# A gated recurrence on one core: the second half's scan of m and tanh moved ahead of z's add and sigmoid

## The reference, cut to what matters

```python
def step(h, x_t):
    fused = jax.nn.sigmoid(jnp.concatenate([x_t, h], axis=-1) @ w_W + w_b)
    hidden_state, output_state = jnp.split(fused, 2, axis=-1)
    memory_state = x_t @ wx_W + wx_b + hidden_state * (h @ wh_W + wh_b)
    h_new = output_state * h + (1.0 - output_state) * jnp.tanh(memory_state)
    return (h_new, h_new)
_, hs = jax.lax.scan(step, h0, xT)
x = x + jnp.swapaxes(hs, 0, 1)
```

## Time and profile before

| what | value |
|---|---|
| time, median of 3 runs | 1808.27 us (1807.4 to 1808.76) |
| the profiled execution | 1807.97 us, its span 1806.1 us |
| granted TensorE clock | 0.998 over the span |
| PE, PEld, DVE, ACT, POOL busy | 99%, 90%, 64%, 46%, 20% of the span |

### The profile page before, as it was taken

How to read it: one execution, slowest core, us unless ns; L and a number is a source line. 1 busy time by engine, 2 the same in 40 slices (tenths; PEclk the granted TensorE clock), 3 DMA queues, 4 the chain that set the end, 5 groups by cost and what they waited for, 6 DMA issues and landing times.

```text
span 1806.1 us, 178513 instructions
## 1 busy us (share of the span) xinstructions
PE 1787.5 (99%) x78208; PEld 1629.9 (90%) x78208; DVE 1160.5 (64%) x6153; ACT 824.9 (46%) x3983; POOL 357.1 (20%) x1540
## 2 busy tenths in 40 slices
PE   7999999999999999999999999999999999999998
PEld 6999999999999999999999999999999999999997
DVE  2666666666666666666666666666666666666665
ACT  2444444444444444444444444444444444444444
POOL 0222222222222222222222222222222222222221
PEclk9999999999999999999999999999999999999999
DMA  6222333223332223332233322233322333223332
GB/s 218 87 67 86 91 91 91 73 75 91 91 91 85 69 86 92 92 92 69 81 92 92 91 77 74 88 91 91 91 68 80 91 91 92 74 74 94 92 92 82
DMA packets 180731, 159.86 MB, mean 89 GB/s; under 512 B 12016, under 2 KB 179440, under 8 KB 180720
## 3 DMA queue, kind: packets, MB, share of 16 engines
q1 hardware_dynamic: 180720, 159.72, 29.6%
HBM read 151.28 MB, written 8.39 MB: 88 GB/s over the span
## 4 chain that ended last, share of the span: by engine, by line
PE 98%; SPq 1%; DMA 0%; issue 0%; DVE 0%; ACT 0%; POOL 0%; POOLq 0%; DVEq 0%
PE ps L232 78%; PE ps L200 20%; SPq L167 0%; SPq L162 0%; DMA x_sb<-in_x 0%; SPq L153 0%; SPq L159 0%; DVE turned L324 0%; SPq L150 0%; DVE h L347 0%; DVE m_pre L338 0%; SPq L157 0%; SPq L156 0%; SPq L155 0%; DVE pre_r L328 0%
## 5 line engine op out<-in xcount | busy, mean ns | idle before, releaser
L232 PE MATMUL ps<-wh,h 128*8 128x128 f32 (+1 forms) x65536 | 1504.7, 246 | 2.6 <-issue 2.2
L232 PEld LDWEIGHTS ps<-wh,h 128*8 128x8 f32 x65536 | 1324.7, 90 | 143.1 <-DVE h L347 113.5
L324 DVE STREAM_TRANSPOSE turned<-ps 128x128 f32<-128x128 f32 (+1 forms) x2048 | 550.4, 269 | 412.4 <-PE ps L232 412.4
L277 ACT ACTIVATE m_by<-pre_r 128x16 f32<-128x16 f32 x1024 | 224.2, 219 | 701.2 <-DVE pre_r L328 701.2
L200 PE MATMUL ps<-x_next,wx_step 128*32 128x128 f32 x12288 | 433.0, 274 | 0.6 <-issue 0.6
L347 DVE TENSOR_TENSOR_SCAN h<-h_by,h 128x48 f32<-128x48 f32 x1024 | 274.2, 268 | 152.4 <-ACT h L286 152.4
L403 POOL TENSOR_TENSOR add<-turned,bias_h 128x16 f32<-128x16 f32 x1024 | 222.8, 218 | 709.9 <-DVE turned L324 681.5
L281 ACT ACTIVATE h_by<-pre_z 128x16 f32<-128x16 f32 x1024 | 229.6, 224 | 249.8 <-DVE pre_z L332 246.0
L200 PEld LDWEIGHTS ps<-x_next,wx_step 128*32 128x32 f32 x12288 | 316.1, 110 | 16.2 <-issue 4.3
L416 POOL TENSOR_TENSOR y<-x_sb,h 128x32 f32 x512 | 134.0, 262 | 734.5 <-DVE h L347 734.5
L286 ACT ACTIVATE h<-m_pre 128x32 f32<-128x32 f32 x1024 | 237.8, 232 | 1.8 <-DVE m_pre L338 1.8
(11 more groups left out here) (8 smaller groups left out, 1.1 us busy)
## 6 DMA issues: line engine op xcount, KB each, us to landing
wx_step<-in_w_x SPq DMA_DIRECT2D x516, 192.0 KB, 2.4
x_next<-in_x SPq DMA_DIRECT2D x132, 256.0 KB, 3.2
x_sb<-in_x SPq DMA_DIRECT2D x34, 256.0 KB, 3.2
out_h<-y SPq DMA_DIRECT2D x32, 256.0 KB, 2.9
wx<-in_w_x SPq DMA_DIRECT2D x6, 512.0 KB, 7.3
wh<-in_w_h SPq DMA_DIRECT2D x4, 768.0 KB, 11.0
bias_x<-in_b_x SPq DMA_DIRECT2D x1, 6.0 KB, 3.2
bias_h<-in_b_h SPq DMA_DIRECT2D x1, 2.0 KB, 3.6
```

Source lines behind the costliest of these rows:

```text
L232: mm = pe.matmul(ps[Q * j:Q * j + B, bank, 0:cols], h_of(s - 1, k), wh[:, k, j, at:at + cols], start=(k == 0), stop=(k == KC - 1), tile_po ...
L277: act.activation(m_by[:, o, :, 1], pre_r[:, o, :], ACT.Sigmoid).then_inc(r_ready[o], 1)
L324: return dve.transpose(turned[:, o, g0:g1].rearrange("p g c q -> p (g c) q"), ps[:, bank, 0:cols].rearrange("p (c q) -> p c q", q=Q))
```

## The change

1. **VectorE, half 1.** `mix_m(1)` goes ahead of the wait for Z_B's transpose and of `sum_z(1)`.
2. **ScalarE, half 1.** `new(1)` (tanh) goes ahead of `update(1)` (z's sigmoid).
3. **VectorE, first transpose.** In every fourth step the wait for RM_A now comes first and that for `y_added` second.
4. **TensorE, x products.** The wait for `x_next_loaded` is gone; SyncE instead waits for x before it loads the slot's weights, and issues x ahead of them, so that the weights' arrival stands for both. One semaphore for emptied banks becomes three, one for each bank, and the values that TensorE waits for are worked out once in 4 steps.
5. **ScalarE, last step of a block.** It waits for three semaphores in place of one, and adds three times in place of once.

```diff
--- before.py
+++ after.py
@@ -130,7 +130,7 @@
         h_ready = halves("h_ready")
         x_placed = sem("x_placed")
         hm_ready = halves("hm_ready")
-        xg_ready = sem("xg_ready")
+        xg_free = [sem(f"xg_free{u}") for u in range(X_UNITS)]
         xg_turned = sem("xg_turned")
 
         y_added = sem("y_added")
@@ -163,8 +163,10 @@
                     .then_inc(wx_step_loaded[s % RING], 16)
 
             for r in range(RING):
+                sp.dma_start(x_next[:, r], x_flat[:, :, TOK:2 * TOK]).then_inc(x_next_loaded[r], 16)
+            for r in range(RING):
+                sp.wait_ge(x_next_loaded[r], 16)
                 load_wx(r)
-                sp.dma_start(x_next[:, r], x_flat[:, :, TOK:2 * TOK]).then_inc(x_next_loaded[r], 16)
             sp.dma_start(x_sb[:, :, TOK:2 * TOK], x_flat[:, :, TOK:2 * TOK]).then_inc(x_loaded, 16)
             with sp.Fori(0, BLOCKS) as i:
                 after = sp.snap((i + 2) % BLOCKS)
@@ -178,9 +180,11 @@
                         sp.wait_ge(x_used[s % RING], turn)
                     else:
                         sp.wait_ge(x_product, sp.snap(i * UNITS + (s // RING + 1) * X_UNITS + UNITS))
+                    if s >= STEPS - RING:
+
+                        sp.dma_start(x_next[:, s % RING], x_flat[:, :, cols]).then_inc(x_next_loaded[s % RING], 16)
+                        sp.wait_ge(x_next_loaded[s % RING], sp.snap(i * 16 + 32))
                     load_wx((s + RING) % STEPS)
-                    if s >= STEPS - RING:
-                        sp.dma_start(x_next[:, s % RING], x_flat[:, :, cols]).then_inc(x_next_loaded[s % RING], 16)
                 sp.wait_ge(y_added, sp.snap(i * STEPS + 2 * STEPS))
                 sp.sem_inc(y_taken, 1)
                 sp.dma_start(out_flat[:, :, bass.ds(sp.snap(i * TOK), TOK)],
@@ -206,18 +210,17 @@
             def first_x_products():
                 for u, k in x_list:
                     if k == 0 and u >= X_UNITS:
-                        pe.wait_ge(xg_ready, u - X_UNITS + 1)
+                        pe.wait_ge(xg_free[u % X_UNITS], u // X_UNITS)
                     if k == 0 and u * WX_PARTS % UNITS == 0:
                         pe.wait_ge(wx_loaded[u * WX_PARTS // UNITS], 16)
                     x_product_of(u, k, wx[:, u, k, :], x_sb[:, k, 0:TOK])
 
-            def x_products(i, s):
-                pe.wait_ge(wx_step_loaded[s], held(pe, i * 16 + 16))
-                pe.wait_ge(x_next_loaded[s], held(pe, (i // (STEPS // RING)) * 16 + 16))
+            def x_products(free, loaded, s):
+                pe.wait_ge(wx_step_loaded[s], loaded)
                 for n in range(X_EACH):
                     u, k = divmod(s * X_EACH + n, KC)
                     if k == 0:
-                        pe.wait_ge(xg_ready, held(pe, i * X_UNITS + (UNITS - X_UNITS + u + 1)))
+                        pe.wait_ge(xg_free[u], free)
                     last = x_product_of(u, k, wx_step[:, s, n, :], x_next[:, s, k, :])
 
                 if s < RING - 1:
@@ -234,10 +237,14 @@
                                        tile_position=(0, Q * j))
                 return mm
 
-            def step(t0, s):
+            def step(i, t0, s):
+                nonlocal loaded, free
                 nxt = held(pe, t0 + (s + 1))
                 pe.wait_ge(h_ready[0], nxt)
                 products(RM_A, 0, s)
+                if s == 0:
+                    loaded = held(pe, i * 16 + 16)
+                    free = held(pe, i + UNITS // X_UNITS)
                 products(RM_B, 0, s)
                 pe.wait_ge(h_ready[1], nxt)
                 products(RM_A, 1, s).then_inc(rm_a_done, 1)
@@ -248,6 +255,7 @@
                 products(Z_B, 0, s)
                 products(Z_B, 1, s).then_inc(z_b_done, 1)
 
+            loaded = free = None
             pe.wait_ge(x0_loaded, 16)
             first_x_products()
             pe.wait_ge(wh_loaded, KC * 16)
@@ -256,8 +264,8 @@
             with nc.Fori(0, T // RING, engines=(mybir.EngineType.PE,), hint_back_edge=True) as i:
                 t0 = pe.snap(i * RING)
                 for s in range(RING):
-                    step(t0, s)
-                    x_products(i, s)
+                    step(i, t0, s)
+                    x_products(free, loaded, s)
 
         @block.scalar
         def _(act):
@@ -266,7 +274,7 @@
                 act.wait_ge(x_product, unit0 + (u + 1))
                 dst = xg[:, which, :, u, :].rearrange("p a t b -> p (a t) b")
                 act.activation(dst, ps[:, X_BANK + u % X_UNITS, 0:TOK].rearrange("p (t b) -> p t b", b=B),
-                               ACT.Identity, bias=bias_x[:, u:u + 1]).then_inc(xg_ready, 1)
+                               ACT.Identity, bias=bias_x[:, u:u + 1]).then_inc(xg_free[u % X_UNITS], 1)
 
             def place_x(which, s):
                 dst = add[:, s % 2].rearrange("p o g i w -> p (o g i) w")[:, :, 1]
@@ -286,28 +294,30 @@
                 act.activation(n_twice, m_pre[:, o, :, 1].unsqueeze(2).to_broadcast([P, HB, 2]), ACT.Tanh)\
                     .then_inc(tanh_ready[o], 1)
 
-            def step(t0, s, this, other, unit0):
+            def step(i, t0, s, this, other, unit0):
                 nxt = held(act, t0 + (s + 1))
                 reset(0, nxt)
                 update(0, nxt)
                 new(0, s, nxt)
                 reset(1, nxt)
+                new(1, s, nxt)
                 update(1, nxt)
-                new(1, s, nxt)
                 for u in X_ENDS[s]:
                     empty(u, other, unit0)
                 if s < S:
                     place_x(this, s + 1)
                 else:
-                    act.wait_ge(xg_ready, unit0 + UNITS)
-                    act.sem_inc(xg_turned, 1)
+                    for p in range(X_UNITS):
+                        act.wait_ge(xg_free[p], held(act, i * (UNITS // X_UNITS) + 2 * (UNITS // X_UNITS)))
+                        act.sem_inc(xg_turned, 1)
                     place_x(other, 0)
 
             act.wait_ge(bias_loaded, 2 * 16)
             act.activation(warm[:, :], bias_h[:, :], ACT.Sigmoid)
             for u in range(UNITS):
                 empty(u, slice(0, 1), 0)
-            act.wait_ge(xg_ready, UNITS)
+            for p in range(X_UNITS):
+                act.wait_ge(xg_free[p], UNITS // X_UNITS)
             place_x(slice(0, 1), 0)
             with nc.Fori(0, BLOCKS, engines=(mybir.EngineType.Activation,), hint_back_edge=True) as i:
                 t0 = act.snap(i * STEPS)
@@ -315,7 +325,7 @@
                 other = bass.ds(act.snap((i + 1) % 2), 1)
                 unit0 = act.snap(i * UNITS + UNITS)
                 for s in range(STEPS):
-                    step(t0, s, this, other, unit0)
+                    step(i, t0, s, this, other, unit0)
 
         @block.vector
         def _(dve):
@@ -351,9 +361,9 @@
             def step(t0, i, s):
                 nxt = held(dve, t0 + (s + 1))
                 par = s % 2
+                dve.wait_ge(rm_a_done, nxt)
                 if s % RING == 0:
                     dve.wait_ge(y_added, held(dve, t0 + (s + STEPS)))
-                dve.wait_ge(rm_a_done, nxt)
                 turn(0, 0, R, Z).then_inc(rm_a_turned, 1)
                 dve.wait_ge(rm_a_turned, nxt)
                 dve.wait_ge(x_placed, nxt)
@@ -370,9 +380,9 @@
                 mix_h(0, s, nxt)
                 dve.wait_ge(z_b_done, nxt)
                 turn(3, 1, Z, GATES).then_inc(z_b_turned, 1)
+                mix_m(1, par, nxt)
                 dve.wait_ge(z_b_turned, held(dve, t0 + (s + 2)))
                 sum_z(1, par, nxt)
-                mix_m(1, par, nxt)
                 mix_h(1, s, nxt)
 
             dve.sem_inc(z_b_turned, 1)
```

More of the change, by code:

```diff
@@ L180, in _ @@
                         sp.wait_ge(x_product, sp.snap(i * UNITS + (s // RING + 1) * X_UNITS + UNITS))
-                    load_wx((s + RING) % STEPS)
                     if s >= STEPS - RING:
                         sp.dma_start(x_next[:, s % RING], x_flat[:, :, cols]).then_inc(x_next_loaded[s % RING], 16)
+                        sp.wait_ge(x_next_loaded[s % RING], sp.snap(i * 16 + 32))
+                    load_wx((s + RING) % STEPS)
                 sp.wait_ge(y_added, sp.snap(i * STEPS + 2 * STEPS))
```

## The result

The changed kernel takes 1821.47 us (1820.68 to 1823.07, 4 runs) against 1808.51 us: a ratio of 1.0072, 95% interval 1.0055 to 1.009, 13.0 us slower. The forecast was 1823.8 us. That the sum came so near is luck, for two errors in it cancel: the tail of the step costs about half of what was forecast (5 us for 10.8), and the start and the end of the kernel, forecast at nothing, cost 4 to 7 us. One of the 16 executions of the kernel before that runs 4, 6, 7 and 8 are set against took 2983.86 us at a granted clock of 0.557; their ratios leave it out, and it lifts the median of those 16 from 1807.75 to 1808.03.

The account below looks back on a forecast made before the run. The prediction took the ring through VectorE and ScalarE as the bound: 1807.97 + 10.8 (tail) + 4.7 (first transpose) = 1823.5, plus 0.3 for the median, 1823.8 us. Range 1806 to 1834 us, leaving out rivals 1 and 3.

Parts of the forecast that it names:

- What bounds: Each step's ring through VectorE and ScalarE sets the time, 512 times; TensorE, though 99% busy, waits for half 1.
- three signs of being wrong: `mix_h` within 0.85 us of Z_B's transpose start (T), `mix_m` later than 0.2 behind it, or fourth steps showing 0.75.
- `mix_m` under the transpose: VectorE, half 1: `mix_m` starts at T+0.172, T being Z_B's transpose start, while that 0.22 us transpose still runs.
- Rival 3: VectorE, half 1: the transpose holds `mix_m` back to T+0.22, 0.05 us a step, 25.6 us: 1849 us; chance 0.05.
- The late wait's price: `mix_h` of half 1: z's late second wait, an EVENT_SEMAPHORE, costs 0.104 us, against 0.033 for an ordinary link.
- Rival 1: `mix_h` of half 1: the late z wait costs only 0.033 us, 25.6 us saved in the tail: 1787 us; chance 0.12.
- The tail's size: Z_B's transpose to `mix_h`, half 1: T+0.860 grows to T+0.881, 0.021 us a step, 10.8 us over 512 steps.
- The first transpose: VectorE, every fourth step: an ALU_OP for `y_added` carries RM_A's wait, 0.84 us behind the last scan; 4.7 us slower.
- Rival 2: First transpose: the register operation goes ahead of the wait, so the swap wins 6.8 us: 1812 us; chance 0.10.
- rival 4: Nothing changes: tail at its low end with the first-transpose swap winning, or 0.01 us less on ScalarE: 1807 us; chance 0.08.
- TensorE's 512 waits: TensorE: 384 waits of 51 ns and 128 of 88 ns go, 30.9 us of its sequencer, counted as nothing.
- SyncE: Transfers: the reordered start loads cost 0 (-1 to +2 us), and waits in the loop stay covered by slots or a block.

Follow-up runs that it names:

- run 4: Kernel before with only the TensorE, SyncE and ScalarE changes, two SyncE issues moved earlier at start and end: 1809.57 us against 1808.03, ratio 1.0009.
- run 6: Kernel before with half 1's VectorE and ScalarE reorders and z's wait named first in half 1's `mix_h`: 1781.09 us against 1808.03, ratio 0.9855.
- run 7: Kernel before with RM_A's wait first and `y_added` counted from 1, needing no register operation: 1801.59 us against 1808.03, ratio 0.9965.
- run 8: Kernel before with the changes of runs 6 and 7 together: 1776.86 us, ratio 0.983; measured again 1777.94 us against 1809.11, ratio 0.9826.
- run 5: Changed kernel with z's wait named before tanh's in half 1's `mix_h`: 1786.76 us against the kernel before's 1809.05, ratio 0.9877.
- run 1: Kernel before with only half 1's `mix_m` and tanh moved ahead of z's add and sigmoid: 1813.98 us against 1809.05, ratio 1.003.
- run 3: Kernel before with only the TensorE, SyncE and ScalarE block-end changes: 1813.08 us against 1809.05, ratio 1.0022.

## Why the prediction was right, point by point

- **What bounds.** Right. In every run but 6 and 8 the first transpose follows the last scan by 0.75 us in ordinary steps, whatever else was changed (from the 21st step on, but for 8 steps of the kernel before and 3 of run 7, at 0.77 to 0.78), and the time follows the tail. TensorE's busy 99% is the same in the slower kernel. None of the three signs of being wrong showed.
- **`mix_m` under the transpose.** Right: T+0.17, while the transpose runs until T+0.22. Rival 3 falls. The Trainium skill, "VectorE: DVE Perf Modes", "The DRAIN you can't avoid", has the next operation wait for the empty pipe, and adds that one that is not held starts earlier; this row, with an overlap of 0.05 us, agrees with the addition and not with the rule.
- **The late wait's price.** Right in size and place: forecast 0.104, measured 0.10 behind z's sigmoid, and 0.03 when the same wait is named first (run 5: from 902.14 + 0.21 to 902.38). Rival 1 falls: it needed under 0.083.
- **The tail's size.** Mis-sized, a term of the sum: 0.021 us a step forecast, 0.010 measured (T+0.870 for T+0.881), and 3.3 to 7.8 us in run 1 where 10.8 stood. The step that failed is z's sigmoid's "its end at T+0.777", taken from a mean of 0.224. It starts 0.007 later than forecast (T+0.560 for T+0.553) and is shorter in its new place: 0.210 on average, and the group's mean is down by 8 ns with only half of its members moved, so some 0.016. So it ends at T+0.770. The last 0.004 are the dear link, 0.100 for 0.104.
- **The first transpose.** Right: 0.84 forecast and measured in every fourth step from the 21st on; 4.7 us forecast, 3.8 measured alone (2.0 to 5.4). That the ALU_OP is to blame, run 7 bears out: without it the same order of waits gives 0.75. Rival 2 falls, and with it rival 4, which needed it.
- **TensorE's 512 waits.** Right that they are worth nothing here: the steady step of run 3 is unchanged.
- **SyncE.** Wrong twice, and it is what saved the sum. At the start "in a time when the queue is full anyway: 0" failed: the load on which the first step hangs was issued 3.4 us later and arrived 2.8 later, and the clock fell behind the idle stretch, 1.1 us more. In the loop "the others with a block" of cover holds for 31 blocks and not for the last one, whose store has nothing behind it: 2.3 to 3.4 us. Alone the two cost 4.0 us (2.4 to 5.6); the range given was -1 to 2.
- **The sum.** The three parts measured alone, 4.9 + 3.8 + 4.0 = 12.7 us, against 13.0 for the whole change. The forecast had 5.9 us too much in the tail, 0.9 too much in the first transpose and 4.0 too little at the ends; that they nearly cancel is luck.

## What to carry to other kernels

Where an instruction has two waits, name first the one that comes last: here the second cost 0.07 us more each time it was late, 34.7 us over 512 steps for a swap of two lines, and a value worked out between them brought the late wait onto a register operation, 0.02 dearer still. Reordering a chain moves the late arrival to another wait, so go through the waits of the consumer each time the order of its producers changes. A wait added to a transfer queue is hidden by the loop only while there is a next turn: cost its first and its last turn by themselves.

## What the runs showed of the hardware that had not been expected

- Two operations are shorter in a place where their input was ready before their engine came to them. z's add of half 1 took 0.15 us behind `mix_m` and 0.18 when it waited for the transpose; the group's mean fell from 176 to 163 ns. z's sigmoid took 0.21 behind tanh and 0.22 when it waited for the add. It is no rule for every operation: tanh took 0.23 us both behind the sigmoid and when it waited for `mix_m`.
- A wait costs by the form that it takes on VectorE: 0.75 us from scan to transpose when the late wait goes with the transpose, 0.82 as an EVENT_SEMAPHORE ahead of it, 0.84 on a register operation.
- Behind a standstill of 5.0 us in the first step (27.8 to 32.8), TensorE's granted clock was 0.66 and 0.77 of full speed in the stretches from 28 to 34 and 34 to 40 us, and 1.00 again from 38 on. In the kernel before it was 1.00 in both, and 0.74 earlier, from 22 to 28 us.
